# Group-norm attention on one core: channel group sums by turned blocks on VectorE instead of products on TensorE

## The reference, cut to what matters

```python
xg = x.reshape(B, H, W, 32, C // 32)                 # 32 groups of 16 channels
mean = jnp.mean(xg, axis=(1, 2, 4), keepdims=True)
var = jnp.var(xg, axis=(1, 2, 4), keepdims=True)
xn = ((xg - mean) * lax.rsqrt(var + 1e-3)).reshape(B, H, W, C) * gamma + beta
xf = xn.reshape(B, 1024, C)
q, k, v = xf @ wq + bq, xf @ wk + bk, xf @ wv + bv
attn = softmax(einsum('bnc,bmc->bnm', q, k) * C ** -0.5)
out = (attn @ v) @ wp + bp
return out.reshape(B, H, W, C) + x
```

## Time and profile before

| what | value |
|---|---|
| median of three runs | 2111.44 us (2108.48 to 2112.1) |
| the profiled execution | 2110.5 us |
| its span | 2108.8 us |
| TensorE busy | 2092.9 us, 99% of the span, 9253 matmuls |
| VectorE busy | 1788.8 us, 85% |
| GpSimd busy | 853.0 us, 40% |
| ScalarE busy | 745.9 us, 35% |
| granted TensorE clock | 0.999 of full |
| DMA | mean 52 GB/s |

### The profile page before, as it was taken

How to read it: one execution, slowest core, us unless ns; L and a number is a source line. 1 busy time by engine, 2 the same in 40 slices (tenths; PEclk the granted TensorE clock), 3 DMA queues, 4 the chain that set the end, 5 groups by cost and what they waited for, 6 DMA issues and landing times.

```text
span 2108.8 us, 28498 instructions
## 1 busy us (share of the span) xinstructions
PE 2092.9 (99%) x9253; PEld 1729.6 (82%) x9253; DVE 1788.8 (85%) x2562; ACT 745.9 (35%) x1220; POOL 853.0 (40%) x463
## 2 busy tenths in 40 slices
PE   8999999999999999999999999999999999999999
PEld 6788888888888888888888888888888888888887
DVE  6998897988988888897988978889898898978965
ACT  5342334324333352332523334233432423325231
POOL 1352433523344342542524435243443434425253
PEclk9999999999999999999999999999999999999999
DMA  6212020120401203012030211203012030120201
GB/s 175 60 36 85 1 91 29 50 70 0 120 0 50 70 10 110 0 50 70 16 105 0 72 48 35 85 0 104 16 50 70 5 115 0 50 70 10 70 1 61
DMA packets 110333, 108.67 MB, mean 52 GB/s; under 512 B 8476, under 2 KB 74016, under 8 KB 110240
## 3 DMA queue, kind: packets, MB, share of 16 engines
q1 hardware_dynamic: 107984, 103.58, 16.3%
q10 hardware_dynamic: 2256, 4.20, 0.7%
HBM read 74.19 MB, written 33.55 MB: 51 GB/s over the span
## 4 chain that ended last, share of the span: by engine, by line
PE 83%; DVE 8%; issue 4%; POOL 2%; ACT 1%; DMA 1%; SPq 1%; DVEq 0%; POOLq 0%; ACTq 0%
PE psum L1245 10%; PE psum L1247 10%; PE psum L1246 10%; PE psum L1267 9%; PE psum L1268 9%; PE psum L1269 9%; PE psum L1071 4%; PE psum L1072 4%; PE psum L1073 4%; PE psum L1151 4%; PE psum L1154 4%; PE psum L1153 4%; POOL total_part L447 1%; DVE pt_lo L679 1%; DVE xn_lo L679 1%
## 5 line engine op out<-in xcount | busy, mean ns | idle before, releaser
L1267 PE MATMUL psum<-v_hi,pt_hi 128*128 128x512 f32 x1024 | 398.5, 389 | 0.0
L1269 PE MATMUL psum<-v_hi,pt_lo 128*128 128x512 f32 x1024 | 398.4, 389 | 0.0
L1268 PE MATMUL psum<-v_lo,pt_hi 128*128 128x512 f32 x1024 | 398.3, 389 | 0.0
L424 POOL TENSOR_TENSOR x_res<-x_res,out_bias 128x512 f32<-128x512 f32 x124 | 191.9, 1572 | 484.0 <-PE psum L1154 368.7
L679 DVE TENSOR_TENSOR pt_lo<-score,pt_hi 128x512 fp32r<-128x512 f32 x256 | 317.3, 1269 | 27.5 <-POOL total_part L447 26.3
L447 POOL TENSOR_TENSOR total_part<-total_part,score 128x512 f32<-128x512 f32 x192 | 299.9, 1562 | 16.6
L570 ACT ACTIVATE score<-psum 128x512 f32<-128x512 f32 x256 | 152.6, 596 | 342.3 <-PE psum L1247 342.1
L1269 PEld LDWEIGHTS psum<-v_hi,pt_lo 128*128 128x128 f32 x1024 | 192.2, 188 | 40.0
L1267 PEld LDWEIGHTS psum<-v_hi,pt_hi 128*128 128x128 f32 x1024 | 192.2, 188 | 39.8
L1268 PEld LDWEIGHTS psum<-v_lo,pt_hi 128*128 128x128 f32 x1024 | 192.2, 188 | 39.8
L1245 PE MATMUL psum<-v_hi,xn_hi 128*128 128x512 f32 x512 | 201.7, 394 | 0.0
(11 more groups left out here) (164 smaller groups left out, 3947.0 us busy)
## 6 DMA issues: line engine op xcount, KB each, us to landing
x_res<-in_x_dram SPq DMA_DIRECT2D x128, 256.0 KB, 2.8
out_dram<-x_res SPq DMA_DIRECT2D x128, 256.0 KB, 2.9
x_blk<-in_x_dram SPq DMA_DIRECT2D x240, 128.0 KB, 3.2
score<-in_x_dram SPq DMA_DIRECT2D x16, 128.0 KB, 7.7
w_q<-in_L_conv_wq_dram SPq DMA_DIRECT2D x1, 1024.0 KB, 5.4
w_k<-in_L_conv_wk_dram SPq DMA_DIRECT2D x1, 1024.0 KB, 7.8
w_v<-in_L_conv_wv_dram ACTq DMA_DIRECT2D x1, 1024.0 KB, 9.0
w_p<-in_L_conv_wp_dram ACTq DMA_DIRECT2D x1, 1024.0 KB, 13.1
```

Source lines behind the costliest of these rows:

```text
L424: last = nc.gpsimd.tensor_tensor(at, at, out_bias[:, first:end], ALU.add)
L1267: nc.tensor.matmul(dst, hi[:, m, queries], v_hi[:, m, :], start=m == 0, stop=False)
L1268: nc.tensor.matmul(dst, hi[:, m, queries], v_lo[:, m, :], start=False, stop=False)
L1269: end = nc.tensor.matmul(dst, lo[:, m, queries], v_hi[:, m, :], start=False, stop=m == NT - 1)
```

## The change

The two group products leave TensorE, and with them the matrix `group_avg`, the semaphores between TensorE and VectorE, the use of PSUM bank 7 by them, and the wait for the variance before the fourth output tile of each image. In their place VectorE aggregates each channel's mean and variance into `moments` (32 columns each, of which four are used and the rest stay zero), turns them by 32 x 32 blocks so that the 16 channels of a group lie side by side in a row, adds them by row sums, takes deviations and squares there, spreads the result over the 16 places, and turns it back. GpSimd's root reads the turned result. All of this is now done right behind `channel_stats`, before the shift of the first half, in each image; in the setup the turn back stands where the EPS addition stood. Apart from that, the low parts of A's block sums in image 0 move from behind the low parts of image 1's input to the low parts of image 0's values, m = 2, 3 and 4. Some small tensors are merged.

```diff
+        ABL_AT = {2: (0, 1), 3: (2,), 4: (3,)}
...
-            nc.gpsimd.memset(group_avg[:], 1.0 / CG).then_inc(s_const, 1)
+            nc.gpsimd.memset(moments[:], 0.0).then_inc(s_const, 1)
...
             def channel_stats(n):
+                if starts(n):
+                    dve.wait_ge(s_const, 4)
                 for k in range(KC):
-                    last = nc.vector.bn_aggr(mv[:, k, :], bn[:, k, :, :].rearrange("p h s -> p (h s)"))
-                last.then_inc(s_stin, 1)
+                    last = nc.vector.bn_aggr(moments[:, :, k], bn[:, k, :, :].rearrange("p h s -> p (h s)"))
+                last.then_inc(s_sv, 1)
 
             def group_variance(n):
-                dve.wait_ge(s_stin, n * 2 + 1)
-                dve.wait_ge(s_stat, n * 2 + 1)
-                nc.vector.tensor_copy(g_mean[:], stat[:, 0:KC])
-                nc.vector.tensor_tensor(dev[:], mv[:, :, 0], stat[:, 0:KC], ALU.subtract).then_inc(s_sv, 1)
-                dve.wait_ge(s_sv, n * STAT_STEPS + 2)
-                nc.vector.tensor_tensor(dev[:], dev[:], dev[:], ALU.mult).then_inc(s_sv, 1)
-                dve.wait_ge(s_sv, n * STAT_STEPS + 3)
-                nc.vector.tensor_tensor(dev[:], dev[:], mv[:, :, 1], ALU.add).then_inc(s_stin, 1)
+                step = n * STAT_STEPS + 1
+                by_group = moments_t[:].rearrange("p s (g c) -> p s g c", c=CG)
+                means, per_channel = by_group[:, 0], [P, SQ // CG, CG]
+                sums = [group_sums[:, n, :].unsqueeze(2).to_broadcast(per_channel) for n in range(2)]
+                of_groups = spread[:].rearrange("p s (g c) -> p s g c", c=CG)
+                dve.wait_ge(s_sv, step + 1)
+                nc.vector.transpose(moments_t[:], moments[:]).then_inc(s_sv, 1)
+                dve.wait_ge(s_sv, step + 2)
+                nc.vector.tensor_reduce(group_sums[:, 0, :], means, mybir.AxisListType.X, ALU.add).then_inc(s_sv, 1)
+                dve.wait_ge(s_sv, step + 3)
+                nc.vector.scalar_tensor_tensor(out=means, in0=sums[0], scalar=-1.0 / CG, in1=means,
+                                               op0=ALU.mult, op1=ALU.add).then_inc(s_sv, 1)
+                nc.vector.tensor_scalar(of_groups[:, 0], sums[0], 1.0 / CG, None, ALU.mult)
+                dve.wait_ge(s_sv, step + 4)
+                nc.vector.tensor_tensor(means, means, means, ALU.mult).then_inc(s_sv, 1)
+                dve.wait_ge(s_sv, step + 5)
+                nc.vector.tensor_reduce(group_sums[:, 1, :], by_group.rearrange("p s g c -> p g s c"),
+                                        mybir.AxisListType.XY, ALU.add).then_inc(s_sv, 1)
+                dve.wait_ge(s_sv, step + 6)
+                nc.vector.tensor_scalar(of_groups[:, 1], sums[1], 1.0 / CG, EPS, ALU.mult, ALU.add).then_inc(s_sv, 1)
 
             def variance(n):
-                dve.wait_ge(s_stat, n * 2 + 2)
-                nc.vector.tensor_scalar(g_var[:], stat[:, 0:KC], EPS, None, ALU.add).then_inc(s_pw_in, 1)
+                dve.wait_ge(s_sv, n * STAT_STEPS + MOMENTS)
+                nc.vector.transpose(group_stats[:], spread[:]).then_inc(s_pw_in, 1)
...
                 if more:
                     channel_stats(b + 1)
+                    group_variance(b + 1)
+                    variance(b + 1)
...
                     top_part_step(b, 1, m)
-                    if more and m == 3:
-                        group_variance(b + 1)
                     if m > 1:
                         pt_lo_parts(b, 0, m - 2, m - 1)
-                if more:
-                    variance(b + 1)
                 pt_lo_parts(b, 0, NT - 2, NT)
                 for m in range(2, NT - 1):
+                    if starts(b):
+                        for n in ABL_AT.get(m, ()):
+                            block_lo(SUMS[n], len(WHOLE) + n + 1, ab_sum[:, SUMS[n]])
                     v_lo_part(b, m)
...
                     xn_lo_parts(b + 1, 0, KC)
-                if starts(b):
-                    for n, at in enumerate(SUMS):
-                        block_lo(at, len(WHOLE) + n + 1, ab_sum[:, at])
...
-            def group_sum(n, step, rhs):
-                pe.wait_ge(s_stin, n * 2 + step + 1)
-                if step == 0 and not (isinstance(n, int) and n < 2):
-                    pe.wait_ge(s_y, (n - 1) * NT)
-                nc.tensor.matmul(stat[:, 0:KC], group_avg[:], rhs, start=True, stop=True).then_inc(s_stat, 1)
...
-                if i == TH - 1 and more:
-                    pe.wait_ge(s_pw_in, n + 2)
...
-            weight_product(SET_M, *parts, 0, 1)
-            group_sum(0, 0, mv[:, :, 0])
-            weight_product(SET_M, *parts, 1, 2)
-            group_sum(0, 1, dev[:])
-            weight_product(SET_M, *parts, 2, KC)
+            weight_product(SET_M, *parts)
...
-                    if more and m == 2:
-                        group_sum(b + 1, 0, mv[:, :, 0])
-                    if more and m == 6:
-                        group_sum(b + 1, 1, dev[:])
```

More of the change, by code:

```diff
@@ L133, in group_norm_attention @@
         ident = sb("ident", [P, P])
-        ones = sb("ones", [P, 1])
-        group_avg = sb("group_avg", [P, P])
+        constants = sb("constants", [P, 1 + KC])
+        ones, minus_half = constants[:, 0:1], constants[:, 1:1 + KC]
         vec_cols = sb("vec_cols", [P, 3 * KC])
         gamma_c, beta_c, bv_c = (vec_cols[:, n * KC:(n + 1) * KC] for n in range(3))
-        minus_half = sb("minus_half", [P, KC])
         wk_bq = sb("wk_bq", [P, KC])
         wq_bk = sb("wq_bk", [P, KC])
-        bqbk = sb("bqbk", [P, 1])
-        bqbk_part = sb("bqbk_part", [P, 1])
+        bias_product = sb("bias_product", [P, 2])
+        bqbk, bqbk_part = bias_product[:, 0:1], bias_product[:, 1:2]
         out_bias = sb("out_bias", [P, C])
@@ L153, in group_norm_attention @@
         bn = sb("bn", [P, KC, NH, 6])
-        mv = sb("mv", [P, KC, 2])
-        g_mean = sb("g_mean", [P, KC])
+        moments, moments_t, spread = (sb(n, [P, 2, SQ]) for n in ("moments", "moments_t", "spread"))
+        group_sums = sb("group_sums", [P, 2, SQ // CG])
+        group_stats = moments_t
+        g_mean, g_var = group_stats[:, 0, 0:KC], group_stats[:, 1, 0:KC]
         dev = sb("dev", [P, KC])
-        g_var = sb("g_var", [P, KC])
         rstd = sb("rstd", [P, KC])
@@ L166, in group_norm_attention @@
         o_ps = [psum[:, 4 + i, :] for i in range(TH)]
-        stat = psum[:, 7, :]
-        vec_ps = stat[:, KC:4 * KC]
+        vec_ps = psum[:, 7, 0:3 * KC]
         last_total = psum[:, 0, 0:TH]
@@ L280, in group_norm_attention @@
         BIAS_PARTS, BIAS_CHAIN, BIAS_STEPS = 3, 4, 5
-        STAT_STEPS = 6
+        MOMENTS, STAT_STEPS = 8, 11
         def lo_rank(u):
@@ L406, in _ @@
                                     pattern=[[-1, P]], channel_multiplier=1).then_inc(s_const, 1)
[L407 to L413, removed]
             def root(n):
                 pool.wait_ge(s_pw_in, n + 1)
-                nc.gpsimd.tensor_tensor(rstd[:], g_var[:], minus_half[:], ALU.pow).then_inc(s_pw, 1)
+                nc.gpsimd.tensor_tensor(rstd[:], g_var, minus_half, ALU.pow).then_inc(s_pw, 1)
             def residual(n, i, first=0, end=C):
@@ L742, in row_part @@
                 if k == 0:
-                    nc.vector.tensor_scalar(by_half(row[:]), x_t[:, :, 0, :], wq_bk[:, 0:1], bqbk_part[:],
+                    nc.vector.tensor_scalar(by_half(row[:]), x_t[:, :, 0, :], wq_bk[:, 0:1], bqbk_part,
                                             ALU.mult, ALU.add).then_inc(s_rv, 1)
@@ L899, in _ @@
                            ((w_k, bq_wide, wk_bq), (w_q, bk_wide, wq_bk)) for k in range(KC)]
-            vector_sums.append((bq_wide[:], bk_wide[:], bqbk[:]))
+            vector_sums.append((bq_wide[:], bk_wide[:], bqbk))
             def sum_products(first, end):
@@ L1248, in score_tile, with out_tile @@
                 last.then_inc(s_work, 1)
-            def out_tile(n, i, more):
+            def out_tile(n, i):
                 h = i // TH
@@ L1274, in out_tile @@
                     for c in range(TH):
-                        summed = nc.tensor.matmul(last_total[:, c:c + 1], total_part[:, chunk(c)], ones[:, 0:1],
+                        summed = nc.tensor.matmul(last_total[:, c:c + 1], total_part[:, chunk(c)], ones,
                                                   start=True, stop=True)
                     summed.then_inc(s_tt, 1)
-            pe.wait_ge(s_const, 6)
+            pe.wait_ge(s_const, 5)
             weight_transpose(SET_WQ, w_q, s_wload[0])
@@ L1314, in image @@
                 for i in range(NT):
-                    out_tile(b, i, more)
+                    out_tile(b, i)
             if B > 1:
```

16 lines of the change are left out of this document (7 added, 9 removed).

## The result

The changed kernel takes 2102.66 us (median of six runs, 2100.86 to 2103.18) against 2111.13 us of the kernel before beside it; the ratio is 0.9960, with a 95% interval of 0.9949 to 0.9971. It is 8.5 us faster by the medians, where 10 were forecast. The profiled execution took 2103.18 us, the slowest of the six, with a span of 2101.4 us, 7.4 us less than before.

The account below looks back on a forecast made before the run. TensorE's issue, busy 99%, was taken as the bound: 2110.5 - 7.3 (products) - 1.2 (A's low parts) - 2.0 (query waits) + 0.2 (setup) = 2100.2 us profiled, 2101 as median; range 2097 to 2107.5.

Parts of the forecast that it names:

- The products: Group products on TensorE in images 0 to 14: removing 30 at 0.243 us each gains 7.3 us, nothing hides it.
- Rival 3: A group product on TensorE costs only its columns, 0.05 us, 1.5 us for all 30: 2107 us; chance 0.02.
- The waits at the queries: TensorE's late query products from image 1 on, 3.9 us with echoes: 2.0 us saved, plus 1.2 us in image 1.
- the lead of 0.5 us for VectorE: Second half's shift starts 0.5 us sooner relative to TensorE, between 1.0 and -0.4, removing nearly all query waits.
- The early all-reduces: GpSimd's root no longer waits for VectorE, so both second-half all-reduces end about 4 us sooner, near 644 to 645.
- their collision with the normalisations: The four normalisations at 640.47 lie beside the earlier all-reduce and end up to 2 us later.
- rival 1: VectorE and GpSimd set the pace at the queries, TensorE's saving returns as waits: 2103.1 to 2109; chances 0.15 and 0.09.
- rival 1 in its first form: Waits at the queries stay as they are: 2103.1 us; with waits as now or a little more, chance 0.15.
- low parts of A's sums: Four VectorE subtractions, 2.48 us, move into idle time among image 0's values; image 1's query wait goes: 1.2 us gained.
- VectorE's chain: Eight steps of 0.2 us, 1.6 us, before the first half's shift, hidden in idle time; price on TensorE 0.
- the doubtful case: GpSimd's all-reduce holds the chain's multiply-add or square by 0.9 us; first half's shift 0.8 us late, bounds 0 and 1.5.
- The setup: Before the loop: TensorE's 1.4 us lead is worth 0, VectorE's longer chain counts: +0.2 us, between -0.5 and +1.0.

Follow-up runs that it names:

- e7: e2 with two 4-column products on constants, read by nothing, put back on TensorE in each image: 2104.73 us.
- e1: Changed kernel with two 4-column products on constants, read by nothing, put back on TensorE at their old places in each image: 2107.61 us.
- e2: Changed kernel with only the turn back, and so GpSimd's root, moved late to where the EPS addition stood: 2098.74 us.
- e3: Changed kernel with the next image's normalisation one value tile earlier, behind the low part of tile 3 instead of 4: 2099.55 us.
- e5: Kernel before with ten long-fulfilled waits (five instructions) at the head of VectorE's stream, nothing else different: 2107.41 us.
- e4: Changed kernel with only the four low parts of A's block sums back behind the low parts of image 1's input: 2105.65 us.
- e9: Kernel before with two long-fulfilled waits (one instruction) at the head of VectorE's stream, the control for e5: 2110.81 us.
- e6: e2 with 240 long-fulfilled waits (120 instructions) at the head of VectorE's stream: 2102.12 us.
- e10: e6 with six waits (three instructions) more at the head of VectorE's stream: 2102.45 us.
- e8: e2 with VectorE's whole chain, not only the turn back, moved to the old one's place in the second half's scores: 2100.34 us.

## Why the prediction was right, and where it was not

**The products** were priced rightly and carry the gain: 0.243 us each, 7.3 us; e7 gives 7.4 between profiled executions and 6.0 between medians. Rival 3, a product for 0.05 us, is refuted by e1 and e7.

**The waits at the queries** were the term that failed. I took 2.0 + 1.2 us off; the trace shows 0.4 us more. Two steps of the prediction led there. (That the total still came out 1.6 us from the forecast is in part luck, as said below.)

First, the lead of 0.5 us for VectorE. The early all-reduces came as forecast, and I had named their collision with the normalisations, but priced it at 2 us from the one scaling that stood beside such an all-reduce. I overlooked the scale step in front of them, four elements from two SBUF operands, held by 2 us, as the same reasoning had it for the multiply-add. Together it is 3.5 us, and the average lag grew by 0.5 us instead of shrinking by 0.5. e2 takes the collision away; e3 starts the normalisations ahead of it, so that what is left of it comes early enough. Both end the late starts of images 2 to 15. The price in the changed kernel is 3 to 4 us: 2102.66 against 2098.74 between medians, 4.3 between spans, 2.7 by the ratios to the kernel before.

Second, the argument against rival 1: "Both engines start anew there, so what TensorE saves before does not shorten VectorE's time to the queries." The wait for ScalarE that I leaned on is still there in the changed kernel (0.9 us in most images, before the scale step), but the hold that follows ends 2.25 to 2.26 us behind the all-reduce's start in all 14 images, however early the step began. In the kernel before, the start of GpSimd's all-reduce hung on the root, and that on VectorE's EPS addition near the end of the second half's scores; the shift hung on this all-reduce in turn. Timeline before, VectorE in image 4, in front of its shift at 649.11:

```profile
646.60 1.16 DVE L870 CUSTOM_DVE_ANT_0 total_part<-total_part,ident 128x128 f32<-128x128 f32 x1 [1.18 <-POOL total_part L456]
```

With the root's wait gone, that start hangs on the first half alone, and TensorE's saved time does shorten VectorE's time to the queries; e1 shows the late starts falling by 3 us when TensorE gets its products back. The outcome is rival 1 in its first form, late starts as now, for which I had 2103.1 us; the measured 2102.66 lies beside it. That closeness is luck too: the figure still takes 1.2 us off for image 1 and adds 0.2 for the setup, where the trace shows 0.4 more late starts and 0.2 less setup. The stated range held the result because it reached there.

**The cause of the late starts before** I had not found. I took VectorE and GpSimd's work for it. From image 2 on it was for the larger part a still stand of VectorE behind its loop's jump, and e5 gains 3.3 us by the medians, 2.7 in the profiled loop, with five idle instructions and none of the change. The change moves the loop by five instructions too, so it removed the still stand by accident. That and the collision about cancel, which is why the late starts look unchanged: this is the luck in the total. The parts depend on each other and do not add up strictly, but by runs they are: products -7.3 us, position -2.7 to -3.3 us, collision +3 to +4 us, low parts of A's sums -1.7 us in image 1 (-0.9 over the loop). That they combine so inside the changed kernel is argued; no run has the change with the loop at its old place.

**The low parts of A's sums** were forecast at -1.2 us with the idle time as cover. e4 gives 1.7 us at the queries of image 1 and 0.9 over the loop. The cover was thin: one of the four is held for 2.5 us in image 0, and the second half's shift there is 3.8 us behind ScalarE's last high part. So TensorE's late start in image 1 only fell from 1.13 to 0.87 us.

**VectorE's chain** was right in its free price (eight steps of 0.2 us), in being held by the all-reduce (0.7 us of delay, 0.8 taken in the doubtful case), and in costing TensorE nothing. The rule of the Trainium skill, SBUF — State Buffer, section Who interferes with whom, says that a step with two SBUF inputs is held till the end of GpSimd's instruction. The trace agrees only in part. The held square ends at 610.66, with the all-reduce (610.63). But the multiply-add ends at 609.92, 0.7 us before that, and the scale step at 639.29 while the all-reduce lasts until 640.28. **The setup** was forecast at +0.2 us and is -0.2, within what it scatters between the kernels that share it (58.2 to 59.1; 58.6 to 60.1 for the setup of the kernel before, in e5 and e9).

## What to carry to other kernels

Read an engine that feeds the bound one for what will run beside what after the move: an engine freed from a wait starts its next work earlier, and here the wait that went was what kept two all-reduces off the normalisation. Before building on a small wait in a loop, look at the instruction queue and at the first instructions behind the loop's jump: if packets recur in every round and an engine stands still there with its inputs long ready, a few idle instructions at its head test it. The best version found, e2, keeps the change and puts only the step that lets GpSimd go back to its old place: 2098.74 us, ratio 0.9947.

## What the runs showed of the hardware that I had not expected

Five idle instructions ahead of a loop of 262 on VectorE took its instruction packets from 78 to 13 and 3.3 us from a kernel that is 99% busy on another engine (e5), while one instruction did not (e9). Refetching in each round costs nothing in one position (e6), and stops the engine by up to 0.7 us three instructions further on (e10).

An all-reduce of the totals on GpSimd holds a four-element step on VectorE by 2 us and lets it go 2.25 to 2.26 us behind its own start, 14 times of 14, about 1 us or more before its recorded end (3.25 to 3.8 us). The shorter one of 1.79 us lets a step go 1.1 us behind its start and the next one at its end. So a hold does not last as long as the all-reduce is recorded. Neither a turn by blocks nor a row sum beside it was held (0.25 and 0.18 to 0.22 us at any place), so of the eight steps only those with two SBUF operands and the scalings were (e8 for the second scaling, 1.07 us).
